# A two-layer attention and mixture-of-experts kernel: batch 0 normalised before the outputs of the sixth quad, weight tiles split earlier, exponentials ahead of the gate copies

## What is computed

```python
mod = (_silu(L0_c) @ L0_wmod).reshape(L0_c.shape[0], 6, 1, -1)
sa, ca, ga, sb, cb, gb = (mod[:, 0], mod[:, 1], mod[:, 2], mod[:, 3], mod[:, 4], mod[:, 5])
h = _layernorm(x, axis=-1) * (1 + ca) + sa
x = x + ga * _L0_attn_ref(h, L0_attn_w_qkv, L0_attn_w_out)
h = _layernorm(x, axis=-1) * (1 + cb) + sb
x = x + gb * _L0_ffn_ref(h, ...)
```

## Time and profile before

| what | us |
| --- | --- |
| median of three runs (670.19 to 679.08) | 671.88 |
| the profiled execution, its own time | 665.51 |
| its span in the profile | 663.7 |
| TensorE matmuls busy | 606.6 |
| VectorE busy | 379.0 |
| ScalarE busy | 302.3 |
| GpSimd busy | 129.3 |

### The profile page before, as it was taken

How to read it: one execution, slowest core, us unless ns; L and a number is a source line. 1 busy time by engine, 2 the same in 40 slices (tenths; PEclk the granted TensorE clock), 3 DMA queues, 4 the chain that set the end, 5 groups by cost and what they waited for, 6 DMA issues and landing times.

```text
span 663.7 us, 10873 instructions
## 1 busy us (share of the span) xinstructions
PE 606.6 (91%) x3897; PEld 471.5 (71%) x3907; DVE 379.0 (57%) x757; ACT 302.3 (46%) x462; POOL 129.3 (19%) x137
## 2 busy tenths in 40 slices
PE   3898899798999999999998897889997999999995
PEld 3777645487788888888886565543445878888884
DVE  6477535966244444544457699792358543345455
ACT  3657275554233333333333473427864643333331
POOL 4501015323122222222230000000112331222220
PEclk9999899999899999999999899898999999999999
DMA  8364454100001111111100024301210001111101
GB/s 324 98 223 173 145 162 153 50 1 25 24 26 48 47 47 47 47 47 47 47 25 0 1 69 133 121 5 62 81 56 25 1 25 47 48 47 47 43 7 63
DMA packets 22194, 44.64 MB, mean 67 GB/s; under 512 B 3632, under 2 KB 7632, under 8 KB 22160
## 3 DMA queue, kind: packets, MB, share of 16 engines
q1 hardware_dynamic: 21840, 44.05, 20.8%
q10 hardware_dynamic: 320, 0.13, 0.1%
HBM read 33.16 MB, written 11.01 MB: 67 GB/s over the span
## 4 chain that ended last, share of the span: by engine, by line
PE 67%; DVE 19%; ACT 4%; issue 4%; DMA 2%; POOL 2%; SPq 0%; DVEq 0%; ACTq 0%; POOLq 0%
PE PS L557 32%; PE PS L980 16%; DVE nmx L1531 5%; PE PS L857 3%; PE PS L827 2%; PE PS L701 2%; PE PS L703 2%; DVE x L1601 1%; PE PS L601 1%; DMA w_raw<-in_wqkv 1%; PE PS L714 1%; DVE stats L1430 1%; DVE xn L1743 1%; ACT q_masked L1129 1%; PE PS L872 1%
## 5 line engine op out<-in xcount | busy, mean ns | idle before, releaser
L1273 ACT ACTIVATE qk_hi<-xn 128x512 fp32r<-128x512 f32 x82 | 51.7, 631 | 171.0 <-DVE xn L1743 139.6
L557 PE MATMUL PS<-h_hi,wqkv_hi 128*128 128x512 f32 x304 | 102.7, 395 | 1.9 <-DVE h_lo L1464 1.3
L557 PE MATMUL PS<-h_hi,wqkv_lo 128*128 128x512 f32 x272 | 92.8, 396 | 2.6 <-DVE xn L1653 2.6
L1740 DVE TENSOR_TENSOR prs<-prs,PS 128x512 f32<-128x512 f32 x60 | 41.2, 687 | 86.8 <-PE PS L557 78.3
L1747 DVE TENSOR_TENSOR qk_lo<-xn,qk_hi 128x512 fp32r<-128x512 f32 x70 | 48.4, 692 | 47.8 <-ACT qk_hi L1273 47.8
L1269 ACT ACTIVATE prs<-PS 128x512 f32<-128x512 f32 x82 | 48.7, 594 | 48.5 <-PE PS L557 48.5
L557 PEld LDWEIGHTS PS<-h_hi,wqkv_hi 128*128 128x128 f32 x304 | 57.2, 188 | 14.0 <-DVE h_lo L1464 1.7
L557 PE MATMUL PS<-h_lo,wqkv_hi 128*128 128x512 f32 x160 | 62.9, 393 | 0.0
L557 PEld LDWEIGHTS PS<-h_hi,wqkv_lo 128*128 128x128 f32 x272 | 51.1, 188 | 14.9 <-DVE xn L1653 4.3
L1531 DVE TENSOR_REDUCE nmx<-PS 128x512 f32 (+4 forms) x96 | 54.2, 637 | 4.4 <-PE PS L719 4.3
L980 PE MATMUL PS<-wqkv_hi,qk_hi 128*128 128x256 f32 x288 | 53.5, 285 | 0.9 <-POOL qk_lo L529 0.7
(11 more groups left out here) (251 smaller groups left out, 1223.4 us busy)
## 6 DMA issues: line engine op xcount, KB each, us to landing
fw_raw<-in_ffn SPq DMA_DIRECT2D x41, 384.0 KB, 3.1
qk_slot<-rows_scr SPq DMA_DIRECT2D x32, 200.0 KB
rows_scr<-qk_hi SPq DMA_DIRECT2D x16, 256.0 KB
qk_slot<-q_scr SPq DMA_DIRECT2D x32, 100.0 KB
rows_scr<-qk_lo SPq DMA_DIRECT2D x8, 256.0 KB
wmod<-in_wmod SPq DMA_DIRECT2D x1, 1536.0 KB, 14.3
x<-in_x SPq DMA_DIRECT2D x2, 512.0 KB, 4.0
wmod<-in_wmod SPq DMA_DIRECT2D x1, 1024.0 KB, 10.8
```

The costliest lines, as they stand in the source:

```text
L557: ins = nc.tensor.matmul(dst, left(a, c), right(b, c), start=n == 0, stop=n == total - 1)
L1273: nc.scalar.activation(hidR[b][0], hid[b], ACT.Copy).then_inc(f["hi"], 1)
L1740: tt(hid[buf] if half is None else gu[buf], gact[buf], PS[:, 5, :], ALU.mult).then_inc(f["gu"], 1)
```

## The change

Six edits, all at or around the two passes over the values:

- SyncE: the loads of weight tiles 2 and 3 move from behind the key loads of heads H + 5 = 21 and H + 10 = 26 to behind those of heads H - 3 = 13 and H + 3 = 19.
- GpSimd: the low parts of tiles 0, 1, 2 move from the ends of quads 2, 3 and 6 to the starts of quads 2, 3 and 4, ahead of that quad's copy of values and low part of outputs. ScalarE: the high part of tile 2 moves from exponential 7n - 2 to 4n - 1.
- TensorE: the wait for the gate copies moves from before unit 2's scores to before quad 0's values; ScalarE copies the gates after two exponentials instead of before the first.
- ScalarE: a tiny exponential (`exp_table`) is put before the high part of batch 1's maxima, and with it the load of the table of exponentials.
- VectorE: `normalise` goes before `outputs(l, BQ + 1)`, and `h_low` before `outputs(l, BQ + 3)`.
- TensorE: chunk 1 of batch 1's projection goes behind `early_up(0)`.

```diff
--- before.py
+++ after.py
@@ -392,8 +392,8 @@
                     sp.wait_ge(at[l][f"mw{b}"], 16 * 2)
                     for u in range(b * H, (b + 1) * H):
                         load_keys_major(l, u)
-                        if u in (H + 5, H + 10):
-                            s = (u - H) // 10
+                        if u in (H - 3, H + 3):
+                            s = u // H
                             load_ffn(l, 1, s, 2 + s)
 
             sp.wait_ge(consts, CONSTS)
@@ -502,13 +502,12 @@
                     pool.wait_ge(v_taken, 2 * B)
                     take_values(0)
                 for g in range(QUADS):
+                    if g in (2, 3, 4):
+                        weights_low(l, g - 2, g % 2)
                     if l == 0 and g + 1 < QUADS:
                         take_values(g + 1)
                     if g % 2:
                         out_low(l, g // 2)
-                    if g in (2, 3, QUADS - 2):
-                        i = min(g - 2, 2)
-                        weights_low(l, i, i % 2)
 
             def weights_low(l, i, s):
 
@@ -843,6 +842,8 @@
                 if blocks[0] == 0:
                     ge(a["oe"], g - (1, 0)[l])
                     if l == 0:
+                        if g == 0:
+                            pe.wait_ge(gate_taken, 2)
                         pe.wait_ge(a["vs"], SLOTS * (g + 1))
                     pe.wait_ge(a["p"], PER_QUAD[l] * (g + 1))
                 for kb in blocks:
@@ -884,8 +885,6 @@
                 for s in range(2):
                     keys_major(l, s)
                 pe.wait_ge(at[l]["mlo"], B)
-                if l == 0:
-                    pe.wait_ge(gate_taken, 2)
                 n = PER_QUAD[l]
                 for j in range(2, n):
                     keys_major(l, j)
@@ -926,6 +925,8 @@
                 zero(Y1_BANK, Y1_BANK + 1)
                 pe.wait_ge(at[l]["ol"], CHUNKS - 1)
                 project_out(l, 1, range(OC - 1), False)
+
+            def out_projection_rest(l):
                 pe.wait_ge(at[l]["ol"], CHUNKS)
                 project_out(l, 1, range(OC - 1, OC), False)
 
@@ -1014,6 +1015,7 @@
 
                 pe.wait_ge(hl_ready, 4 * n + 2)
                 early_up(0)
+                out_projection_rest(l)
                 early_up(1)
                 logits(l, 0)
                 zero(0, 1)
@@ -1140,6 +1142,9 @@
                     for s in range(SLOTS):
                         mask_q(l, b, g, s)
 
+            def exp_table():
+                nc.scalar.activation(table_in[:, :], ct[:, 0, 0, 0:1], ACT.Exp)
+
             def max_high(l, b):
 
                 a = at[l]
@@ -1184,6 +1189,7 @@
             take_v(1)
             max_high(0, 0)
             mask_rest(0, 1)
+            exp_table()
             max_high(0, 1)
 
             def exponentials1(j):
@@ -1208,7 +1214,6 @@
                     return
             def attention(l):
                 if l == 0:
-                    gates(0)
                     act.wait_ge(split, 3)
                 n = PER_QUAD[l]
                 for u in range(n * QUADS):
@@ -1216,8 +1221,10 @@
                         exponentials1(u)
                     else:
                         exponentials(l, u)
-                    if u in (2 * n - 1, 3 * n - 1, 7 * n - 2):
-                        i = u // n - 1 if u < 4 * n else 2
+                    if l == 0 and u == 1:
+                        gates(0)
+                    if u in (2 * n - 1, 3 * n - 1, 4 * n - 1):
+                        i = u // n - 1
                         weights_high(l, i // 2, i % 2)
 
             def take_rows(l):
@@ -1627,11 +1635,11 @@
                 aggregate = gate_and_add(l, 0, 0, 1, Y0_BANK[l][1])
                 aggregate()
                 norm_scales(n, slice(0, 1))
+                normalise(n)
                 outputs(l, BQ + 1)
-                normalise(n)
                 outputs(l, BQ + 2)
+                h_low(n, 0)
                 outputs(l, BQ + 3)
-                h_low(n, 0)
                 dve.wait_ge(y_ps, 4 * l + 3)
                 first = gate_and_add(l, 0, 1, 0, Y1_BANK)
                 dve.wait_ge(y_ps, 4 * l + 4)
```

## The result

The changed kernel takes 698.48 us (median of four executions, 692.78 to 711.29) where the kernel before, run beside it, took 675.02 (670.19 to 679.08). The ratio is 1.0387, with a 95% interval of 1.0326 to 1.0448: slower. The profiled execution took 696.6 us with a span of 694.8, against 665.51 and 663.7 before, so the two profiles are 31.1 us apart; the mean granted clock fell from 0.984 to 0.955. The ratio speaks of 26 us, the two medians are 23.5 us apart. All are in one direction, and the differences between the numbers are part of the finding: much of what was lost is TensorE's clock, and that isn't the same in every execution.

The account below looks back on a forecast made before the run. TensorE carried two thirds of the chain, VectorE a fifth; SyncE's weight loads were expected to decide. Layer 0 +10.9 and layer 1 +10.0 made +20.9 us, added to the 671.88 median: 692.8 us, range 684 to 698.

Parts of the forecast that it names:

- the stops: Both layers: TensorE waits for head 14's keys, queued behind SyncE's load of tile 2; +8.2 us layer 0, +6.4 layer 1.
- the gain of 1.0 us at the start: Layer 0's pass start: table load in ScalarE's idle time, exponentials before gate copies; third exponential at 83.10 instead of 84.09.
- The tail of layer 1: End of layer 1's pass: quad 6's values wait for VectorE's transpose, now behind normalising; +2.2 us, bounds 1 and 3.
- The clock: TensorE behind the stop in each layer: about 3.0 us at 1.2 GHz, costing 1.5 us each, bounds 0 and 1.5.
- So +1.6: End of layer 0's pass: last values wait for GpSimd's later copy, second chunk starts later; +1.6 us, bounds 0 and 2.3.
- one stop only: Rival: layer 1's stop fails to come because its quads are longer; +13.0 us, 684.9 us, chance 8%.
- no stop: Rival: head 14's keys land in time, the queue having run a round of slots ahead; +2.9 us, 674.8 us, chance 5%.
- A clock that doesn't fall: Rival: the forecast without the 3.0 us of clock, 689.8 us; counted into the forecast's own range, no separate chance.

## Why the prediction was wrong in size

Right were the stops: 8.2 and 6.4 us predicted, 8.1 (8.6 less the 0.45 by which the pass began later) and 6.1 in the profile, both ended by the keys of head 14, behind SyncE's load of tile 2, behind GpSimd's first split. The run with the weight tiles undone takes both away and lands where the theory put it; the weight tiles alone bring them back. Right was the gain of 1.0 us at the start (34.77 to 33.81). The tail of layer 1, 2.2 against 2.4, agrees in part by luck. Its cause is there, but quad 6's wait grew from 0.66 us to 1.96, 1.3 us and not 2.3; the rest came behind it, with the clock at 0.90 and 0.67 in the windows from 520 and 524. The stretch from quad 6's values to the second chunk takes 15.0 us there (521.91 to 536.90) and 13.6 at 1.00, in the run with the product's wait filled (498.09 to 511.67). Without these 1.4 us the tail would be 1.0 us longer than before, not 2.2.

The step that failed is the one headed "The clock": "I take 1.5 for each stop, bounds 0 and 1.5". It measured 2.0 and 4.5. The 1.5 was worked out from one window of the earlier trace rows with a mean of 0.62, as if a fall always lasted those 3.0 us. Behind layer 1's stop it lasted from 488 to about 499 with TensorE busy, and filling the stops gave back some 7 us by the ratios, with a wide interval, where the term held 3.0. One observed fall is a sample and no bound.

The same omission stands in the tail. "So +1.6" for layer 0 treated the wait for VectorE's first product as a wait alone: it named its cause rightly (the product stands behind both gate-and-adds, which follow the second chunk), and saw that nothing is won by the tile. But a wait of 3.15 us in front of the densest stretch of the kernel has a clock behind it: 1.5 us in layer 0 and 4.7 in layer 1 in the profile, and 0 in the prediction. The run with that wait filled shows that it is the clock, since the wait stays. Layer 0's tail was 1.3 us more than predicted besides, and this is mostly the clock as well. The last values waited 3.00 us for the copy on GpSimd, which took 1.86 us and not the 1.28 of the earlier trace rows (135.30 to 137.16); even so they began, counted from the last scores, only 1.3 us later than before, where 1.65 was predicted. Then they took 2.41 us for 1.40, with 0.69 and 0.89 in the windows from 136 and 140, and from them to the second chunk it was 7.6 us where the prediction had 5.9 and the run with the wait filled has 6.7 (126.38 to 133.06).

Together the clock's terms make up 2.0 + 1.5 + 4.5 + 4.7 - 1.2 = 11.5 us of the profile where 3.0 were predicted: 8.5 of the 10.2 us by which the sum was short. The some 0.9 and 1.4 us inside the two tails come on top, so that what isn't the clock came out slightly below its prediction. The upper end of the range, 698, rests on the bound of 1.5 for each stop; with a bound taken from the 4.5 the result would have been well inside. That it lay only half a microsecond under the result is no merit of the sum: the executions of the changed kernel themselves run from 692.78 to 711.29 us.

The rivals: one stop only, and no stop, fell, since both came. A clock that doesn't fall was named and given its price; what was missing is its counterpart, a clock that falls longer and oftener than in the one sample. Nor does that sample fit the reading that a fall follows an idle TensorE: in the 4 us from 450 it was busy for 3.83 us, and its longest wait in the ten before was 0.54 us (443.83).

By the Trainium skill ("TensorE: Matmul & The Clock Gate", "HAM oscillation — how this bites in real kernels") an idle gap of TensorE costs more than its length, because the array then starts at the lower clock. The runs with filled waits agree in kind: 0.997 against 1.0141. The section's own example has 1.67 us at the lower clock for each gap; the changed kernel's rows have some ten microseconds behind one, and there the rows decide.

## What to carry to other kernels

Before a load that waits is moved forward in a queue, read what the loads behind it feed and when that is wanted: the keys here weren't late until a weight load stood before them, and moving the load without the split cost 54 us. When an operation is moved ahead on one engine, move its consumer on the next engine too, here VectorE's first product, which one line put right. And price a wait of TensorE by what it runs next: if that is dense, the same wait can cost its length plus several microseconds more at half clock, which fillers can hold off when the wait itself can't be removed.
